# Three fp32r matmuls in place of one fp32 matmul in the two dense layers of a graph-network kernel

## The reference, cut to what matters

```python
def _mlp(x, W1, b1, W2, b2, W3, b3):
    a = jax.nn.leaky_relu                      # slope 0.01
    x = a(x @ W1 + b1)
    x = a(x @ W2 + b2)
    return a(x @ W3 + b3)
for _ in range(3):                             # u starts as x
    v = _mlp(adj @ u, uv_W1, uv_b1, uv_W2, uv_b2, uv_W3, uv_b3)
    u = _mlp(adj @ v, vu_W1, vu_b1, vu_W2, vu_b2, vu_W3, vu_b3)   # the last u is not used
x = layernorm(x + v)
x = layernorm(x + adj @ (x @ gcn_W))
```

## Time and profile before

| | |
|---|---|
| time, three runs | 1230.63 us median (1228.97 to 1234.26) |
| span of the profiled execution | 1227.7 us (its own time is not listed apart from these three) |
| TensorE, share of the span busy | 98% (1204.8 us) |
| TensorE weight loads | 79% |
| VectorE | 81% (1000.3 us) |
| ScalarE | 72% (879.7 us) |
| DMA | 397.32 MB, mean 324 GB/s |
| mean granted TensorE clock | 0.997 of full speed |

### The profile page before, as it was taken

The page is one execution under the profiler, slowest core; times in us unless marked ns, Lnnn a source line. Parts: engine busy times, 40 slices in busy tenths (PEclk is TensorE's granted clock), DMA queues, the critical chain, the costliest instruction groups (busy, mean ns, idle before and its releaser), DMA issues.

```text
span 1227.7 us, 16097 instructions
## 1 busy us (share of the span) xinstructions
PE 1204.8 (98%) x5376; PEld 968.1 (79%) x5376; DVE 1000.3 (81%) x624; ACT 879.7 (72%) x695; POOL 11.0 (1%) x29
## 2 busy tenths in 40 slices
PE   6999999999999999999999999999999999999997
PEld 5888778877887878778877887787877778788886
DVE  5888888888888878888888888888888878787884
ACT  5677777777777767777777777778777777777773
POOL 2000000000000000000000000000000000000000
PEclk9999999999999999999999999999999999999999
DMA  8999988798989789988878989978888886898992
GB/s 326 372 354 342 362 338 334 281 344 346 344 337 346 274 302 340 352 340 341 333 290 340 343 338 347 346 273 325 300 317 312 310 320 232 311 371 344 364 361 92
DMA packets 55474, 397.32 MB, mean 324 GB/s; under 512 B 6449, under 2 KB 6577, under 8 KB 7441
## 3 DMA queue, kind: packets, MB, share of 16 engines
q1 hardware_dynamic: 54576, 394.88, 85.1%
q0 software_dynamic: 864, 1.97, 0.4%
HBM read 394.73 MB, written 2.10 MB: 323 GB/s over the span
## 4 chain that ended last, share of the span: by engine, by line
PE 96%; ACT 2%; DMA 1%; issue 1%; DVE 1%; SPq 0%; ACTq 0%; DVEq 0%
PE acc L553 84%; PE layer L496 6%; PE proj L502 3%; PE minus_mean L514 1%; ACT high L242 1%; PE var L520 1%; DMA resid<-x_t_dram 1%; PE spread L534 1%; ACT squared L276 0%; DVE low L371 0%; ACT L269 0%; ACT centered L265 0%; ACT p_high L246 0%; ACT std L269 0%; DVE p_low L404 0%
## 5 line engine op out<-in xcount | busy, mean ns | idle before, releaser
L371 DVE TENSOR_TENSOR low<-raw,high 128x2048 fp32r<-128x2048 f32 x372 | 842.2, 2290 | 184.7 <-ACT high L242 184.2
L242 ACT ACTIVATE high<-raw 128x2048 fp32r<-128x2048 f32 x372 | 712.4, 1916 | 80.4 <-PE acc L553 65.7
L553 PE MATMUL acc<-high,p_low 128*128 128x512 f32 x1536 | 643.3, 419 | 7.5 <-issue 3.1
L553 PE MATMUL acc<-low,p_high 128*128 128x512 f32 x1536 | 600.9, 391 | 0.0
L553 PE MATMUL acc<-high,p_high 128*128 128x512 f32 x1536 | 600.1, 391 | 0.0
L553 PEld LDWEIGHTS acc<-high,p_low 128*128 128x128 f32 x1536 | 289.0, 188 | 87.1 <-issue 28.8
L553 PEld LDWEIGHTS acc<-high,p_high 128*128 128x128 f32 x1536 | 289.1, 188 | 79.4 <-issue 22.8
L553 PEld LDWEIGHTS acc<-low,p_high 128*128 128x128 f32 x1536 | 288.6, 188 | 61.8
L376 DVE SCALAR_TENSOR_TENSOR h<-z 128x512 f32<-128x512 f32 x120 | 82.6, 689 | 0.0
L257 ACT ACTIVATE z<-layer,b_uv_b 128x512 f32<-128x512 f32 x48 | 33.1, 690 | 68.2 <-PE layer L496 68.2
L246 ACT ACTIVATE p_high<-proj 128x512 f32 (+1 forms) x40 | 23.8, 598 | 65.1 <-PE proj L502 65.1
(11 more groups left out here) (46 smaller groups left out, 264.2 us busy)
## 6 DMA issues: line engine op xcount, KB each, us to landing
raw<-adj_dram SPq DMA_DIRECT2D x372, 1024.0 KB, 5.2
kept<-adj_dram SPq DMA_DIRECT2D x2, 1024.0 KB, 8.3
resid<-x_t_dram SPq DMA_DIRECT2D x1, 1536.0 KB, 9.1
out_t_dram<-z POOLq DMA_DIRECT2D x3, 256.0 KB, 4.9
out_t_dram<-normed POOLq DMA_DIRECT2D x3, 256.0 KB, 5.1
resid<-x_t_dram SPq DMA_DIRECT2D x1, 512.0 KB, 5.1
out_t_dram<-z SPq DMA_DIRECT2D x1, 256.0 KB, 2.0
out_t_dram<-normed SPq DMA_DIRECT2D x1, 256.0 KB, 2.0
```

Of the source, the lines that this page charges most:

```text
L242: nc.scalar.activation(high[slot][:], source[:], ACT.Copy).then_inc(high_ready, 1)
L371: nc.vector.tensor_tensor(low[slot][:], source[:], high[slot][:].bitcast(F32), ALU.subtract).then_inc(low_ready, 1)
L553: done = nc.tensor.matmul(acc[side][:], part[parity][:, at:at + D], adj_part[slot][:, columns], start=(g == 0 and j == 0 and i == 0), stop ...
```

## The change

The weights W2 and W3 of both networks are split once into `w_high` (ACT) and `w_low` (DVE), between the splits of step 0 and the first tail. In each tail the activation `h` is split before layers 2 and 3: ACT copies it to `h_high` (`raise_h`, straight behind the bias), DVE subtracts to get `h_low` (`lower_h`, straight behind the leaky ReLU). PE does three fp32r matmuls, `w_low` with `h_high`, `w_high` with `h_high`, `w_high` with `h_low`; the first waits for `h_high`, the third for `h_low`. `KEPT` goes from 2 to 1, so that one more group is loaded for chunk 0 in each of the last five products. In the norm tails the third layer stands behind group 3 (before: 2), `center` behind 5 (4), `variance` behind 6 (5), the spread of the deviation behind 7 (6); the projection stays behind 6.

```diff
-KEPT = 2
+KEPT = 1
+LAYERS = ["uv_W2", "uv_W3", "vu_W2", "vu_W3"]
-NORM_LAYER_2_AT, NORM_LAYER_3_AT, NORM_CENTER_AT, NORM_VAR_AT, NORM_PROJECT_AT, NORM_SPREAD_AT = 1, 2, 4, 5, 6, 6
+NORM_LAYER_2_AT, NORM_LAYER_3_AT, NORM_CENTER_AT, NORM_VAR_AT, NORM_PROJECT_AT, NORM_SPREAD_AT = 1, 3, 5, 6, 6, 7
...
 # ACT
+            def split_weights():
+                act.wait_ge(consts_loaded, N_CONSTS)
+                act.wait_ge(consts_set, CONSTS_SET)
+                for name in LAYERS:
+                    nc.scalar.activation(w_high[name][:], w[name][:], ACT.Copy).then_inc(w_high_ready, 1)
+            def raise_h(step, k):
+                act.wait_ge(h_ready, step * 3 + k - 1)
+                nc.scalar.activation(h_high[:], h[:], ACT.Copy).then_inc(h_high_ready, 1)
...
                 first_bias(step, side, way)
+                raise_h(step, 2)
                 ahead(0, LAYER_2_AT + 1)
                 later_bias(step, 2, way)
+                raise_h(step, 3)
                 ahead(LAYER_2_AT + 1, LAYER_3_AT + 1)
...
 # DVE
+            def lower_h(step, k):
+                dve.wait_ge(h_high_ready, step * 2 + k - 1)
+                nc.vector.tensor_tensor(h_low[:], h[:], h_high[:].bitcast(F32),
+                                        ALU.subtract).then_inc(h_low_ready, 1)
...
                 leaky(step, 1)
+                lower_h(step, 2)
                 ahead(0, LAYER_2_AT + 1)
                 leaky(step, 2)
+                lower_h(step, 3)
                 ahead(LAYER_2_AT + 1, LAYER_3_AT + 1)
...
 # PE
-                pe.wait_ge(h_ready, step * 3 + k - 1)
-                nc.tensor.matmul(layer[:], weight[:], h[:], start=True,
+                pe.wait_ge(h_high_ready, step * 2 + k - 1)
+                nc.tensor.matmul(layer[:], w_low[name][:], h_high[:], start=True, stop=False)
+                nc.tensor.matmul(layer[:], w_high[name][:], h_high[:], start=False, stop=False)
+                pe.wait_ge(h_low_ready, step * 2 + k - 1)
+                nc.tensor.matmul(layer[:], w_high[name][:], h_low[:], start=False,
                                  stop=True).then_inc(layer_done, 1)
```

More of the change, by code:

```diff
@@ L83, in gnn_kernel @@
         w = {name: sbuf(f"w_{name}", [D, D]) for name in WEIGHTS}
+        w_high = {name: sbuf(f"w_high_{name}", [D, D], F32R) for name in LAYERS}
+        w_low = {name: sbuf(f"w_low_{name}", [D, D], F32R) for name in LAYERS}
         b = {name: sbuf(f"b_{name}", [D, 1]) for name in BIASES}
@@ L91, in gnn_kernel @@
         h = sbuf("h", [D, CHUNK])
+        h_high = sbuf("h_high", [D, CHUNK], F32R)
+        h_low = sbuf("h_low", [D, CHUNK], F32R)
         centered = sbuf("centered", [D, CHUNK])
@@ L114, in gnn_kernel @@
         z_ready = sem("z_ready")
+        w_high_ready = sem("w_high_ready")
+        w_low_ready = sem("w_low_ready")
         h_ready = sem("h_ready")
+        h_high_ready = sem("h_high_ready")
+        h_low_ready = sem("h_low_ready")
         layer_done = sem("layer_done")
@@ L339, in _ @@
                 split(g, g % SLOTS, loads_of(0, 0, g), kept_of(0, g))
-            act.wait_ge(consts_loaded, N_CONSTS)
-            act.wait_ge(consts_set, CONSTS_SET)
+            split_weights()
             with act.Fori(0, ROUND_TRIPS) as trip:
@@ L377, in leaky, with split_weights @@
                                                op0=ALU.mult, op1=ALU.max).then_inc(h_ready, 1)
+            def split_weights():
+                for i, name in enumerate(LAYERS):
+                    dve.wait_ge(w_high_ready, i + 1)
+                    nc.vector.tensor_tensor(w_low[name][:], w[name][:], w_high[name][:].bitcast(F32),
+                                            ALU.subtract).then_inc(w_low_ready, 1)
+            def lower_h(step, k):
+                dve.wait_ge(h_high_ready, step * 2 + k - 1)
+                nc.vector.tensor_tensor(h_low[:], h[:], h_high[:].bitcast(F32),
+                                        ALU.subtract).then_inc(h_low_ready, 1)
             def project_low(step, chunk, side, parity):
@@ L492, in _, with dense @@
         def _(pe):
-            def dense(weight, step, k):
-                pe.wait_ge(h_ready, step * 3 + k - 1)
-                nc.tensor.matmul(layer[:], weight[:], h[:], start=True,
+            def dense(name, step, k):
+                pe.wait_ge(h_high_ready, step * 2 + k - 1)
[3 more added lines that the diff above has]
+                nc.tensor.matmul(layer[:], w_high[name][:], h_low[:], start=False,
                                  stop=True).then_inc(layer_done, 1)
@@ L563, in round_step @@
                 groups(0, LAYER_2_AT + 1)
-                dense(w[f"{way}_W2"], step - 1, 2)
+                dense(f"{way}_W2", step - 1, 2)
                 groups(LAYER_2_AT + 1, LAYER_3_AT + 1)
-                dense(w[f"{way}_W3"], step - 1, 3)
+                dense(f"{way}_W3", step - 1, 3)
                 groups(LAYER_3_AT + 1, PROJECT_AT + 1)
@@ L576, in norm_step @@
                 groups(0, NORM_LAYER_2_AT + 1)
-                dense(w["uv_W2"], step - 1, 2)
+                dense("uv_W2", step - 1, 2)
                 groups(NORM_LAYER_2_AT + 1, NORM_LAYER_3_AT + 1)
-                dense(w["uv_W3"], step - 1, 3)
+                dense("uv_W3", step - 1, 3)
                 groups(NORM_LAYER_3_AT + 1, NORM_CENTER_AT + 1)
@@ L616, in _ @@
             pe.wait_ge(consts_set, CONSTS_SET)
+            pe.wait_ge(w_low_ready, len(LAYERS))
             with pe.Fori(0, ROUND_TRIPS) as trip:
```

## The result

| | before | after |
|---|---|---|
| median | 1229.8 us (4 runs) | 1299.4 us (4 runs, 1296.33 to 1301.23) |
| profiled execution | span 1227.7 us | span 1298.1 us, its time 1299.85 us |
| ratio to before | | 1.0552, 95% interval 1.0531 to 1.0572 |

The change made the kernel 5.5% slower; 1295 us was forecast, with a range of 1274 to 1316.

The account below looks back on a forecast made before the run. DVE with ACT was to replace PE as the bound. 48.4 + 32 x 25.58 + 7 x 30.9 = 1083.3; with 3.2 at the end, the span was 1292.2; plus 2.9, 1295 us, range 1274 to 1316.

Parts of the forecast that it names:

- The bound moves to the cycle of DVE and ACT: Round steps: DVE with ACT becomes the bound, 1.10 us per step above before; PE waits about 1.5 us in each.
- The hand-over: Layers 2 and 3: leaky ReLU, ACT's copy and split, then DVE's split start, 3.34 us in all, before 0.61.
- A round tail: DVE's whole round: two waits on ACT's copy and split, eight splits, third leaky ReLU and `p_low`: 25.58 us, before 24.48.
- 0.7 us in hand for split 10: Tightest load under `KEPT = 1`: lands at 20.8, split by 22.7, DVE wants it at 23.4; counted at nothing.
- the rival with 8%: Loads become a link of the cycle: 6.5 us each, DVE 0.6 us late per round step, 19 us more, 1314 us; 8%.
- a sign named in advance: In the profile after, loads appearing as releasers in the middle of the run would mean the prediction is wrong.
- PE's saving: Dense layers: three fp32r matmuls take 0.68 us against 0.87 for fp32, saving 0.19 per layer, 15 us for 80.
- A norm tail: From first leaky ReLU to the normed result's end on DVE, 30.9 us, 3.6 more than before for each.
- The bare stretch: Norm tails, between reciprocal and `p_low`: no split now hides ACT's four repeats (1.25 us) and four `p_high` (1.02).
- The start: Four 128x128 weight splits on DVE, 1.04 us, precede the first leaky ReLU: 48.4 in place of 47.3.
- The end: Behind the last norm tail: next split starts 30.35 us after its leaky ReLU, before 27.12, so 3.2 more; 178.6 us stay.
- The rule of the Trainium skill: Engine queues: PE can pull weight loads forward; ScalarE and VectorE take instructions strictly in order, so splits queue behind the copy.

Follow-up runs that it names:

- the wait without the work: Kernel with three fp32r matmuls on two fixed tiles and no activation splits, plus ACT's waits for `h` where the copies stood: 1272.27 us, ratio 1.0355.
- half loads: Changed kernel, loading only the first half of each group's columns after chunk 0 of the first product: 1289.46 us, ratio 1.0468.
- the norm order alone: Kernel before with only the norm tails' places changed to 1, 3, 5, 6, 6, 7: 1233.65 us, ratio 1.0030.
- the copies moved: Changed kernel with `h_high`'s copy on ACT and `h_low`'s subtraction on DVE behind the first split of each pair: 1249.13 us, ratio 1.0128.

## Why the prediction was right, point by point

- **The bound moves to the cycle of DVE and ACT.** Shown from four sides. The same work in another order gives 24.04 us round tails; the wait without the work costs 47 us; PE's matmuls exchanged for the fp32 one change nothing; without the splits PE bounds.
- **The hand-over.** 3.34 us forecast, 3.19 and 3.27 measured. The copy, the one duration not in the trace before, costs 0.54 us to the next split's start (0.59 taken). `h_low` is covered, as forecast.
- **A round tail.** The 25.80 of the table is a mean over 32 intervals, and two of them aren't like the others: the first (27.93 us from leaky ReLU to leaky ReLU) and the one in which the outer loop turns (29.70). The other 30 take 25.60 on average, against 25.58 forecast. That is near for two reasons that cancel, which is luck. The hand-overs alone make 25.3 (half loads), 0.3 less than forecast. The loads add 0.3, and the forecast counted them at nothing, with 0.7 us in hand for split 10. Its load is issued 15.57 us into the tail shown above, as forecast, but takes 5.9 us to land there, not 5.2, as the chain of this kernel shows (start, us, what),

```profile
580.37 5.85 DMA raw<-adj_dram
```

and DVE waits 0.30 us for that split. This was the rival with 8%: the mechanism is there, at about half its size (10 us by the half loads, 19 given). It was also a sign named in advance: the prediction called itself wrong "if the loads appear as releasers in the middle of the run", and they do (at 586.32 in the tail shown above), 63 times with 46.1 us, where before it was 16 times with 14.5. So this term of the sum was wrong, though the bound was not.

- **The loop's turn.** The forecast has no term for it. DVE waits there for nothing but the issue,

```profile
462.49 0.69 DVE L377 SCALAR_TENSOR_TENSOR h<-z 128x512 f32<-128x512 f32 x1 [3.69 <-issue]
```

and the interval is 4.1 us above the 25.58 of the others. It was there before as well, by DVE's rows of the kernel before, 27.89 us in place of 24.48:

```profile
437.27 0.68 DVE L376 SCALAR_TENSOR_TENSOR h<-z 128x512 f32<-128x512 f32 x1
...
465.16 0.68 DVE L376 SCALAR_TENSOR_TENSOR h<-z 128x512 f32<-128x512 f32 x1
```

The prediction put it, unseen, into its 27.3 us per norm tail before; by DVE's leaky ReLUs these take 27.10 (832.31 to 1021.98, seven of them).

- **PE's saving.** Mis-sized: 0.22 us per layer by the cadence, not 0.19. The starts around a single layer gave too little; two cadences, 24.48 and 24.03, give it over many steps.
- **A norm tail.** 30.9 forecast, 30.46 measured. Of the 0.4 us too many, 0.2 are the two hand-overs and 0.2 the stretch from the reciprocal to `low` of split 10 (4.52 forecast, 4.35 measured, 896.35 to 900.70). The step that is only half right is its reason. The bare stretch is there (2.49 us), but with the old places the tails are no faster (30.34): another wait, with a slower clock behind it, takes its place. It costs nothing without the hand-overs (27.00 us).
- **The start.** The forecast saw the weight splits, 1.1 us on DVE, and missed what waits for them: PE is held ahead of step 1 until `w_low` is done, 4.7 us, although the weights are used two groups later. It cost 3 us in the first interval. The weight splits themselves took DVE 0.8 us (46.52 to 47.33), and the first leaky ReLU came no later than before only because the split ahead of them began 0.8 us earlier in this execution (44.31, before 45.11): a match by luck.
- **The end.** 3.2 us more forecast, 5.3 measured, because PE's 12 matmuls of the last group ran at half the clock (below).
- **The sum, 1299.4 for 1295.** The four misses of the span are +7.1 (round tails), -3.1 (norm tails), -1.1 (first leaky ReLU) and +2.9 (end and rest), unrounded 5.9 in all. Of the +7.1, 4.1 are the loop's turn, 2.4 the first interval and 0.6 the 30 others. Around the span the forecast added 2.9 us, the distance of the median before from one span; each run of the changed kernel has 1.6 to 1.8 there, and the median lies 0.45 below the profiled run. That takes 1.6 of the 5.9 back. The mechanism held; that the total came within 4.4 us is in part luck, since misses of either sign cancelled.
- **The rule of the Trainium skill**, in "TensorE: Matmul & The Clock Gate", Part 1, that ScalarE takes its instructions strictly in order: the run with waits and no work bears it out. Splits stood behind a wait for `h` that they didn't need, 195 us in all.

## What to carry to other kernels

An engine with a fifth of its time idle can still be the next bound: add up one round of its own order with every hand-over in it, and compare that with the period, before you give it a wait. Put a small step that waits for another engine behind a big one that doesn't; here that alone was worth 50 us. When two costs hide each other, take both away at once, or each experiment will say that its part is harmless, as the norm order did here. And look for the places that come once per run, the start, a loop's turn, the end: they made most of this forecast's miss.

## What the runs showed of the hardware

PE's clock fell to its lower level of 1.2 GHz (0.5 granted) at places where PE had stood still, and PE then paid a second time. In the changed kernel it waited 4.61 us for the last `p_low`, by its timeline

```profile
1113.16 0.79 PE L574 MATMUL acc<-high,p_low 128*128 128x512 f32 x1 [4.61 <-DVE p_low L417]
```

and the stretches behind, with columns PE, PEld, DVE, ACT, POOL busy, PEclk, DMA share and GB/s, are

```profile
1113.00:1119.00 6.00, 5.84 (x15) 4.57 (x16) 2.40 (x2) 0.98 (x2) 0.00 (x0) 0.50 0.54 194
1119.00:1125.00 6.00, 6.00 (x28) 4.99 (x27) 4.39 (x4) 3.53 (x2) 0.00 (x0) 0.98 0.36 112
```

The group took until 1118.5, 5.3 us in place of 2.7. The same came with the norm order alone (granted 0.50 over the 4 us behind a wait of 4.41 us), and in part behind the wait for `w_low` (0.64 over the next 4 us). It also came behind shorter waits, 1.87 us with the old norm places and 0.52 and 1.41 us close together with the copies moved (0.57 over 4 us behind both, shown above). Before, PE stood still for 3.05 us where the outer loop turns, with nothing but the issue to wait for, and the clock stayed at 1.00 behind it. After, it was 3.58 us at the same place, and 0.72 were granted over the next 6 us:

```profile
438.80:444.00 5.20, 5.16 (x23) 4.26 (x24) 1.89 (x2) 1.92 (x1) 0.00 (x0) 1.00 0.97 375
460.00:466.00 6.00, 5.53 (x17) 4.46 (x18) 1.71 (x3) 2.79 (x3) 0.00 (x0) 0.72 0.78 299
```

The first of these rows is of the kernel before, the second of the changed one. What makes the loop's turn longer in some kernels (27.1 to 30.7 us for that interval) wasn't tried and stays open.
